# Marks of present edges scattered ahead of the edge counts, in a graph attention and linear attention layer

## The reference

```python
# graph branch, for each of 3 layers, 4 heads of 192 (x1 = relu(norm(x) @ W_ah))
h = (x1 @ W).reshape(N, 4, 192)
as_n, ad_n = (h * a_src).sum(-1), (h * a_dst).sum(-1)
e = leaky_relu(as_n[src] + ad_n[dst], 0.2)
m = segment_max(e, dst); p = exp(e - m[dst])
out = segment_sum(p / segment_sum(p, dst)[dst] * h[src], dst)
graph = relu(concat(relu(out of 3 layers)) @ W_out + b_out)
# mix branch: 12 heads of 64, 256 random features
q, k, v = norm(x) @ w_qkv.T
k' = exp(k @ proj - |k|^2/2 - max over all) + eps;  q' likewise, max per row
mix = (q' @ (k'.T @ v)) / (q' @ sum(k')) @ w_proj.T + b_proj
x2 = x + mix + graph;  then a switch layer of 8 experts with capacity 195
```

## Time and profile before

| what | value |
|---|---|
| median of 3 runs | 1711.12 us |
| the profiled execution's own time | 1709.37 us |
| span of the profile | 1707.6 us |
| granted clock of PE, mean | 0.962 |
| PE busy | 1541.5 us (90%) |
| DVE busy | 1149.2 us (67%) |
| ACT busy | 681.4 us (40%) |
| POOL busy | 410.1 us (24%) |

### The profile page before, as it was taken

The page is one execution under the profiler, slowest core; times in us unless marked ns, Lnnn a source line. Parts: engine busy times, 40 slices in busy tenths (PEclk is TensorE's granted clock), DMA queues, the critical chain, the costliest instruction groups (busy, mean ns, idle before and its releaser), DMA issues.

```text
span 1707.6 us, 25848 instructions
## 1 busy us (share of the span) xinstructions
PE 1541.5 (90%) x10083; PEld 1186.8 (70%) x10109; DVE 1149.2 (67%) x2629; ACT 681.4 (40%) x1359; POOL 410.1 (24%) x251
## 2 busy tenths in 40 slices
PE   3989999999878789998999989998999999986987
PEld 2556666555444568988888988888888976656664
DVE  6677664105567989999987787668766833885323
ACT  3420001122233366877777763346434621441110
POOL 3688888888500000000000000000000000002331
PEclk9989999999989899999999999999999999986999
DMA  9435545464752514324420354236413224545951
GB/s 342 97 64 113 111 84 122 71 93 75 190 187 87 143 42 120 88 90 114 125 71 28 104 166 162 96 126 197 129 38 103 82 68 153 213 181 203 319 158 50
DMA packets 196620, 213.72 MB, mean 125 GB/s; under 512 B 81551, under 2 KB 149789, under 8 KB 196498
## 3 DMA queue, kind: packets, MB, share of 16 engines
q1 hardware_dynamic: 119874, 187.01, 34.6%
q0 software_dynamic: 75760, 22.70, 8.8%
q10 hardware_dynamic: 864, 2.36, 0.4%
HBM read 144.74 MB, written 68.40 MB: 125 GB/s over the span
## 4 chain that ended last, share of the span: by engine, by line
PE 45%; DVE 19%; POOL 17%; DMA 9%; issue 7%; ACT 3%; SPq 1%; POOLq 0%; ACTq 0%; DVEq 0%
PE bank L1085 17%; POOL table L2142 17%; DVE junk L1503 5%; PE bank L913 4%; PE bank L911 4%; PE bank L912 4%; PE bank L1261 4%; DMA table<-amount,place 3%; PE bank L1249 3%; DVE eb L1538 2%; DVE eb L1547 2%; PE bank L1145 2%; DMA table<-zero 2%; PE bank L1117 1%; PE bank L1102 1%
## 5 line engine op out<-in xcount | busy, mean ns | idle before, releaser
L1085 PE MATMUL bank<-hb,eb 128*128 128x193 f32 (+3 forms) x2400 | 418.8, 332 | 14.5 <-ACT node L1945 9.2
L1085 PEld LDWEIGHTS bank<-hb,eb 128*128 128x128 f32 (+3 forms) x2400 | 399.5, 191 | 20.6 <-issue 10.5
L2142 POOL DMA_INDIRECT table<-amount,place x170 | 345.2, 2030 | 74.4 <-issue 49.1
L2148 POOL IOTA iota8i<- 128x8 int32 x1 | 0.1, 140 | 941.7 <-DMA node_rows<-node 941.7
L1538 DVE SCALAR_TENSOR_TENSOR eb<-shift_b,as_low,shift_b 128x640 f32<-128x640 f32 (+1 forms) x240 | 196.4, 860 | 0.3 <-PE bank L1085 0.2
L1931 ACT ACTIVATE eb<-eb,asd 128x640 f32<-128x640 f32 (+1 forms) x240 | 181.5, 812 | 28.9 <-DVE eb L1538 28.9
L1547 DVE SCALAR_TENSOR_TENSOR eb<-eb,count 128x1280 f32<-128x1280 f32 (+1 forms) x120 | 174.6, 1455 | 2.3 <-ACT eb L1931 2.3
L1503 DVE CUSTOM_DVE_ANT_0 junk<-ab,absent 128x1250 bf16<-128x1250 f32 x120 | 174.3, 1453 | 1.5
L911 PE MATMUL bank<-w_o_hi,aT_hi 128*128 128x384 bf16 (+1 forms) x360 | 119.1, 331 | 0.0
L911 PE MATMUL bank<-wg_hi,x1T_hi 128*128 128x384 bf16 (+3 forms) x360 | 118.9, 330 | 0.1
L913 PE MATMUL bank<-w_o_hi,aT_lo 128*128 128x384 bf16 (+1 forms) x360 | 119.0, 330 | 0.0
(11 more groups left out here) (280 smaller groups left out, 2965.9 us busy)
## 6 DMA issues: line engine op xcount, KB each, us to landing
w<-in_w SPq DMA_DIRECT2D x16, 1152.0 KB, 12.5
shift_b<-shift_rows SPq DMA_DIRECT2D x24, 625.0 KB, 5.8
h_rows<-h_row SPq DMA_DIRECT2D x27, 388.0 KB
hb<-h_rows SPq DMA_DIRECT2D x12, 873.0 KB
ar<-node_rows SPq DMA_DIRECT2D x27, 384.0 KB
table<-zero POOLq DMA_DIRECT2D x3, 3054.0 KB, 21.7
tab<-table SPq DMA_DIRECT2D x27, 312.5 KB, 3.6
qk_rows<-qk_row SPq DMA_DIRECT2D x12, 625.0 KB
```

The costliest lines, as they stand in the source:

```text
L1085: ins = T.matmul(bank[w // 2][0:M, c0:c0 + GC + 1], p[0:K, u, w * P:w * P + M], hv[0:K, t, 0:GC + 1], start=opens and u == 0 and w % 2 == ...
L2142: G.indirect_dma_start(tables[i], bass.IndirectOffsetOnAxis(place[:, c:c + 1], axis=0), amount16[:, c:c + 1], None, compute_op=ALU.add).th ...
```

## The change

Three new DRAM tables `marks` (bf16) are filled with -3e38 and get a plain indirect write of 0 at every edge, with source and destination exchanged, from `place_` on POOL; the self loops are one strided DMA. `absent` is then the elementwise maximum of the three, loaded by SP (`absent_in`) from step 6 of the projections on; ACT's conversion and PE's transposes of the counts go. The accumulating scatters follow as a new step `scatter` after the whole first order, `tab_in` moves from SP to POOL, and the counts are added at mix feature 78 of 138. Edge maxima run from the `v` steps on (rate 1.8, 0.4 beside `qk`, 0.9 in the mix), attention starts after the counts (0.8 and 0.77 items per step), and the dummy matmuls in the mix are gone (those around the top stay).

```diff
+MARKS_AT, COUNTS_AT = 6, 78
+COUNT_RATE, VALUE_EDGE_RATE, KEY_EDGE_RATE, MIX_EDGE_RATE, ATTENTION_RATE = 1.0, 1.8, 0.4, 0.9, (0.8, 0.77)
...
     yield from paced((key_steps(), 1), (tiles, 1), (first_nodes(), 1))
+    for q in range(PIECES):
+        yield "scatter", q
...
 def graph_steps(done):
+    yield "ab_in", 0
+    for _ in range(MARKS_AT):
         yield None
+    yield from in_step([(1, lambda t: [("absent", t)]), (0, lambda t: [("absent_in", t)])], NT)
     edges = edge_steps(done)
+    yield from spread(edges, lambda: (MIX_EDGE_RATE if "projected" in done else KEY_EDGE_RATE if "products" in done
+                                      else VALUE_EDGE_RATE), lambda: "counts" in done)
+    while "counts" not in done:
+        yield None
+    yield from paced((in_step([(1, lambda t: [("count", t)]), (0, lambda t: [("tab_in", t)])], NT), COUNT_RATE))
     yield "head_in", 0
+    yield from paced((attention_steps(done), lambda: ATTENTION_RATE["mixed" in done]), (edges, lambda: MIX_EDGE_RATE))
...
     def features(n):
-        if "open" not in done:
-            yield "warm_mix", 2
+        if n == COUNTS_AT:
+            done.add("counts")
...
 # DVE, place_: one more address
+                V.scalar_tensor_tensor(mark_moved[:, cs], amount[:, cs], LATER, mark_s[:, cs], ALU.is_lt, ...
+                V.tensor_scalar(mark_at[:, cs], mark_moved[:, cs], spare[:, 0:1], None, ALU.add) ...
...
 # DVE, absent_
+                V.tensor_tensor(absent[0:R, t, :], absent[0:R, t, :], others[0], ALU.max) ...
+                V.tensor_tensor(absent[0:R, t, :], absent[0:R, t, :], others[1], ALU.max) ...
...
 # POOL, place_
+                if q == 0:
+                    ge.wait_ge("marks_set", 32)
+                    G.dma_start(marks[2]..., fill...).then_inc(sem["table_zero"], 16)
+                    G.dma_start(marks[0][0:N * (N + 1), :]...[:, :, 0:1], none..., allow_slow_non_contiguous=True) ...
+                if 4 <= q < 4 + TABLES:
+                    G.dma_start(tables[q - 4]..., zero...).then_inc(sem["table_zero"], 16)
+                ge.wait_ge("placed", 2 * q + 1)
                 for c in range(q * CP, min((q + 1) * CP, CHUNKS)):
+                    if i == 0:
+                        ge.wait_ge("marks_set", 48)
+                    ge.wait_ge(f"marked{i}", 16 * added(c, i))
+                    G.indirect_dma_start(marks[i], bass.IndirectOffsetOnAxis(mark_at[:, c:c + 1], axis=0),
+                                         none[0:EP, 0:1], None).then_inc(sem[f"marked{i}"], 16)
...
 # POOL, new steps: scatter(q) holds the accumulating indirect DMAs of before; tab_in(t) is
+                ge.wait_ge("absent_done", NT)
+                for i in range(TABLES):
+                    ge.wait_ge(f"scatter{i}", 16 * added(CHUNKS, i))
+                ge.wait_ge("counted", TABLES * (t - 1))
+                for j in range(TABLES):
+                    G.dma_start(tab[t % 2][j][0:R, :], tables[j]...).then_inc(sem[f"tab_in{t % 2}"], 16)
...
 # SP, absent_in(t)
+                for i in range(TABLES):
+                    sy.wait_ge(f"marked{i}", 16 * added(CHUNKS, i))
+                sy.wait_ge("absent_done", t - 1)
+                for j, into in enumerate((absent[0:R, t, :], *(b[0:R, :].bitcast(BF16) for b in tab[t % 2][0:2]))):
+                    S.dma_start(into, marks[j]...).then_inc(sem[f"marks_in{t % 2}"], 16)
```

More of the change, by code:

```diff
@@ L238, in product @@
         n, c = divmod(m, NC)
-        if m == COUNTS_AT:
-            done.add("scattered")
+        if m == 0:
+            done.add("products")
         if c == 0 and n + 2 < 2 * PAIRS:
@@ L565, in program @@
         tables = [dram(f"table{i}", (P * TABLE[0] * TABLE[1], 1), U16) for i in range(TABLES)]
+        marks = [dram(f"marks{i}", (P * MARKS[0] * MARKS[1], 1), BF16) for i in range(TABLES)]
         h_rows = dram("h_rows", (LAYERS, N, GH, HW))
@@ L612, in program @@
         spare_i, spare = put("spare_i", [EP, 1], I32), put("spare", [EP, 1])
+        key_s, mark_s = put("key_s", [EP, CHUNKS]), put("mark_s", [EP, CHUNKS])
+        mark_moved, mark_at = put("mark_moved", [EP, CHUNKS]), put("mark_at", [EP, CHUNKS], U32)
+        fill = put("fill", [P, MARKS[1]], BF16)
         assert cursor[0] <= after_count
@@ L1055, in warm_last @@
                 keep_warm(4, n)
[L1057 to L1068, removed]
             def gather(i):
@@ L1276, in vector_program @@
             ve = Waits(engine, sem)
+            V.memset(fill[:, :], -BIG).then_inc(sem["set_up"], 1)
             V.memset(zero[:, :], 0.0).then_inc(sem["set_up"], 1)
@@ L2099, in edges_in @@
             def edges_in(_):
-                ge.wait_ge("set_up", 1)
+                ge.wait_ge("set_up", 2)
                 for b, (t0, t1) in enumerate(BATCHES):
                     ge.wait_ge(f"x_in{b}", 16 * (t1 - t0))
-                none = zero[:, :].bitcast(U16)
-                for table in tables[0:2]:
-                    G.dma_start(table.rearrange("(p t n) o -> p t (n o)", p=P, n=TABLE[1]),
-                                none[:, 0:TABLE[1]].unsqueeze(1).broadcast_to([P, TABLE[0], TABLE[1]])
-                                ).then_inc(sem["table_zero"], 16)
+                for table in marks[0:2]:
+                    G.dma_start(table.rearrange("(p t n) o -> p t (n o)", p=P, n=MARKS[1]),
+                                fill[:, :].unsqueeze(1).broadcast_to([P, MARKS[0], MARKS[1]])).then_inc(sem["marks_set"], 16)
                 G.memset(halves[:, :], 1.0).then_inc(sem["pool_set"], 1)
@@ L2130, in place_ @@
             def place_(q):
+                none = zero[:, :].bitcast(BF16)
                 if q == 0:
-                    G.dma_start(tables[2].rearrange("(p t n) o -> p t (n o)", p=P, n=TABLE[1]),
+                    ge.wait_ge("marks_set", 32)
+                    G.dma_start(marks[2].rearrange("(p t n) o -> p t (n o)", p=P, n=MARKS[1]),
+                                fill[:, :].unsqueeze(1).broadcast_to([P, MARKS[0], MARKS[1]])
+                                ).then_inc(sem["table_zero"], 16)
+                    G.dma_start(marks[0][0:N * (N + 1), :].rearrange("(p r s) o -> p r (s o)", p=EP, s=N + 1)[:, :, 0:1],
+                                none[0:EP, 0:N // EP].unsqueeze(2), allow_slow_non_contiguous=True
+                                ).then_inc(sem["marks_set"], 16)
@@ L2141, in place_, with scatter @@
+            def scatter(q):
+                ge.wait_ge("placed", 2 * q + 2)
+                for c in range(q * CP, min((q + 1) * CP, CHUNKS)):
+                    i = table_of(c)
+                    ge.wait_ge("table_zero", 16 * (TABLES + 1))
                     ge.wait_ge(f"scatter{i}", 16 * added(c, i))
@@ L2252, in tab_in @@
                 for i in range(TABLES):
-                    sy.wait_ge(f"scatter{i}", 16 * added(CHUNKS, i))
-                sy.wait_ge("counted", TABLES * (t - 1))
-                for j in range(TABLES):
-                    S.dma_start(tab[t % 2][j][0:R, :],
-                                tables[j][t * P * N:(t * P + R) * N, :].rearrange("(p n) o -> p (n o)", p=R)
-                                ).then_inc(sem[f"tab_in{t % 2}"], 16)
+                    sy.wait_ge(f"marked{i}", 16 * added(CHUNKS, i))
+                sy.wait_ge("absent_done", t - 1)
+                for j, into in enumerate((absent[0:R, t, :], *(b[0:R, :].bitcast(BF16) for b in tab[t % 2][0:2]))):
+                    S.dma_start(into, marks[j][t * P * N:(t * P + R) * N, :].rearrange("(p n) o -> p (n o)", p=R)
+                                ).then_inc(sem[f"marks_in{t % 2}"], 16)
             def ab_in(lh):
```

108 lines of the change are left out of this document (47 added, 61 removed), and 2 rows, old and new, of the table TAKEN_OVER.

## The result

The changed kernel takes 1823.55 us (median of 4 runs, 1821.27 to 1827.64), the kernel before 1710.8 beside it (4 runs): ratio 1.0667, 95% interval 1.0640 to 1.0694. The forecast was 1767, with a range up to 1815: the sign was right, the time lies 57 us above the forecast and 8.5 above the range.

The account below looks back on a forecast made before the run. PE was taken to bind up to 455 us and from 975 to 1435, DVE from 646 to 975. Blocks ending 56 us later made span 1707.6 + 56 = 1763.6, forecast 1767 us with run offsets; range 1685 to 1815.

Parts of the forecast that it names:

- Part 3: Accumulating count scatters on POOL start after the marks, cost 404 us as today, end at 740; first addition at 746 us.
- Part 1: Marks on POOL: first at 63, 170 x 1.5 = 255 us plus 18 for three fills, ending at 336 us.
- Part 2: `absent` and projections: no loss for marks before about 344 us; mix starts at 562 instead of 578, 16 us gained.
- DVE blocks POOL: Rival, 5%: edge maxima hold up POOL's count scatters for 1.45 us each; counts 152 us later, time 1919 us.
- Part 4: Mix without attention: 78 features at 51 us a pair take 170 us, reaching feature 78 at 732, before the counts.
- clock term: In the mix before attention, a low granted clock on PE adds 4.5 us a pair.
- Part 5: Adding counts and opening attention: ten tiles take 38 us, to 784; first gather at 802 against 646.
- Part 6: After the first gather: 666 us of PE work and 23 idle; blocks end at 1491 instead of 1435, 56 us later.
- The faster one: Rival, 20%: late counts are hidden behind mix features; counts at 678, first gather at 741, time 1691 us.
- A plain scatter at 2.03 us: Rival, 9%: plain mark writes cost POOL as much as accumulating ones; marks end at 477, first gather 940, time 1905 us.

Follow-up runs that it names:

- fourth experiment: Changed kernel with the three zero fills of the count tables issued by SP instead of POOL: 1816.1 us, ratio 1.0617 to the kernel before.
- first experiment: Changed kernel with the marks taken up at step 17 instead of 6, removing the wait of the `v` steps: 1815.6 us, ratio 1.0614 to the kernel before.
- third experiment: Changed kernel with no edge maxima beside the scatters, all run after the counts: 1904.9 us, ratio 1.1136 to the kernel before.
- last experiment: Dummy matmuls put back into mix features 0 to 77: changed kernel 1818.4 us; kernel before with attention held back to feature 78, 1728.7 us.

## Why the prediction was wrong

**The step that failed is Part 3**, "They cost what they cost today, ... 404 us": the count scatters took 459 us. Before it the 18 us for three fills in **Part 1** were too few, and the marks ended 26 us late. The two delays sum to 81 us on the chain that sets the first gather. The marks' end at 362 lay just within the bounds given for it (300 to 363); the 404 us had no bounds. By itself the late end of the marks would have left the time inside the range (1767 + 26 = 1793).

*Part 1, marks.* The first mark starts at 58.7 (63 forecast), a mark takes 1.187 us, mean 1.230 (1.2 forecast), and 170 with their issue take 209.1 + 46.1 = 255.2 (255 forecast). But the last one ends at 362, not 336. The term for the fills was 18; from 58.7 to 362 there remain 362 - 58.7 - 255.2 = 48. Of these 45.0 are waits for marks before, and the three longest behind the fills stand behind one fill each (timeline of POOL, the answer to the earlier trace rows):

```profile
128.45 1.19 POOL L2133 DMA_INDIRECT marks<-zero,mark_at  x1 [11.54 <-DMA marks<-zero,mark_at]
149.64 1.19 POOL L2133 DMA_INDIRECT marks<-zero,mark_at  x1 [8.58 <-DMA marks<-zero,mark_at]
172.74 1.19 POOL L2133 DMA_INDIRECT marks<-zero,mark_at  x1 [9.78 <-DMA marks<-zero,mark_at]
```

Together 29.9, where I had let the scatters in flight hide part of an 8.4 us fill; they hid none. The other 15 us are short waits that the kernel before, whose scatters come every 2.3 us, had less of. Issuing by SP (fourth experiment) won back 12 us of the 26.

*Part 2, `absent` and projections.* The marks came 18 us past the 344 up to which `v` loses nothing, and the standstill grew:

```profile
370.33 0.81 DVE L1481 TENSOR_TENSOR absent<-absent,tab 128x1250 bf16<-128x1250 bf16 x1 [54.40 <-DMA tab<-marks]
```

The last `v` tile is at 406.6 (373.9 before), and the mix starts at 585.5, 7 us later than before instead of 16 earlier. The products themselves ran as forecast (PE busy 102 of 108). The first experiment removes the wait and gets 560.2, against 562 forecast: the 16 us exist. They are worth next to nothing here, since the features have to wait for the counts.

*Part 3, counts.* From 362 to 821, 459 us instead of 404. By the groups' rows it was 345.2 busy + 49.1 issue + 12.3 waits = 406.6 (the prediction's 404 takes off 2.6 for a first wait of 4.0 us), and is 375.1 + 46.9 + 36.8 = 458.8: 29.9 more of busy time, 24.5 more of waits for scatters into the same table, 2.2 less of issue. The busy part is the rival "DVE blocks POOL" in small: third experiment, 29 us, not the 152 of a full block. I had dismissed it by `wa_tmp`, an instruction of 0.355 us; an edge maximum takes 1.45 and slows a scatter by 0.17 on the mean. The Trainium skill ("SBUF — State Buffer", "Who interferes with whom") says that a DVE instruction with two SBUF inputs contends with a GpSimd instruction that reads SBUF. The trace agrees in the direction, at a fifth of a full block's price (29/152); that it is this contention and no other hold of the maxima on POOL, no run here tells. The waits stay without the maxima, and their cause is open. 19.4 of the 36.8 us fall before 415 us, where SP brings in 30 loads of marks for `absent`; the DMA share from 375 to 455 is 0.73 (before 0.58, with 1.7 us of such waits from 358 to 415). But no run took these loads away. In the first experiment they fall at the same time (363.8 to 403.1 us, here 363.6 to 402.7), as they wait for the marks in both; there the waits before 415 were 17.0 us, and it is the later ones that fell, from 17.4 to 9.3.

*Part 4, the mix without attention.* Feature 78 was reached at 758 us, 173 after the mix start (170 forecast). The sum and the clock term were right, the spread was not: the three pairs took 44.7, 48.4 and 55.4 us (51 each forecast; first k exponents at 587.5, 632.2, 680.6 and 736.0), and the nine features behind them 24.9 instead of 17.1, as the granted clock sank to 0.70 and 0.57. With the dummies back (last experiment) the stretch is 15.8 us shorter, 4.7 a pair, where I had added 4.5. As the prediction said of this part, it decided nothing: the counts came 63 us later. The q features are 2.26 us apart (620.52 and 622.78, the answer to the earlier trace rows) where 2.18 was taken:

```profile
620.52 0.69 DVE L1558 TENSOR_REDUCE q_max<-bank 128x2 f32<-128x512 f32 x1
621.24 0.16 DVE L1563 SCALAR_TENSOR_TENSOR q_shift<-q_max,diag 128x2 f32<-128x2 f32 x1
621.42 1.44 DVE L1491 CUSTOM_DVE_ANT_0 junk<-ab,absent 128x1250 bf16<-128x1250 f32 x1
...
622.78 0.69 DVE L1558 TENSOR_REDUCE q_max<-bank 128x2 f32<-128x512 f32 x1
```

*Part 5, additions and opening.* From the last scatter's end on POOL 8 us to the first addition (6), 35 for ten tiles (38), 16 to the first gather (18): right. POOL's issue of a load is 0.55 us, not 0.86.

*Part 6, after the opening.* 668 us instead of 689: 654.1 of PE work (666 forecast) and 13.9 idle (23). That DVE is relieved and PE fills up was right, and more so than I gave it. The tail takes 1825.8 - 1548 = 278 us instead of 272.6; counted from the same matmul of block 3 (1548.95, before 1433.33) it is 276.9 against 274.3, so half of the 5 us is where the edge was drawn.

The sum over: the opening +78 (26 and 55 from the scatters, -3 from Part 5), -21 from Part 6, +5 of tail: 1763.6 + 62 = 1825.6, and the span is 1825.8. That 81 us of delay became 62 is luck: Part 6 was priced 21 too high.

**The rivals.** The faster one needed counts at 678; even with plain writes they came at 695, and the kernel stayed slower than before, by 1.3 to 3.8%. A plain scatter at 2.03 us did not occur. The range failed because its upper end, 1815, was built from marks, additions and idle; the longest term of the chain, 404 us of scatters moved beside other work, stood in it as a constant. With the measured 55 us of Part 3 beside the others' ends the range would have reached to 1870.

## What to carry to other kernels

When a long chain of small transfers is put behind another and moved to where other engines are busy, price each one by that neighbourhood, and give the chain's length a range of its own: a tenth of 404 us was more than the 29.5 us of idle time that the sum booked as won. Ask of a late input what stands in order behind the instruction that waits for it; here one addition of counts held DVE, ACT and PE for some 70 us. And before reordering around a slow operation, see whether it has a cheaper kind: a write for an addition gave 0.6% by dropping one argument, with nothing moved. It serves only where no address comes twice in a table.

## What the runs showed of the hardware

- An indirect DMA of 125 two-byte elements keeps POOL 1.19 us as a plain write and 1.99 as an accumulating one (medians), each with some 0.27 of issue.
- Beside edge maxima on DVE (1.45 us, two inputs from SBUF) the mean of the accumulating one rises from 2.034 to 2.207 us, while its median stays.
- A 3 MB fill holds up the small indirect DMAs behind it by 8.6 to 11.5 us. Beside three such fills from SP's queue, issued from 76.1 to 94.3 us, there was no such wait, but 14 short ones of 21.7 us in all.
- With PE at a granted clock of 0.84, 0.81 and 0.70 (563 to 646, to 700, to 750) 78 mix features took 173.4 us; with dummy matmuls that brought it to 0.94, 1.00 and 1.00 they took 157.6.
